# Attention 0 of a two-layer adaLN transformer: splits moved to GpSimd, a token-major output projection, and layer norm at the end of a step

## What is computed

```
mod = silu(c) @ wmod          # sa, ca, ga, ... one vector of 128 per batch
ga  = sign(ga) * max(|ga|, 0.25)
h = layernorm(x) * (1 + ca) + sa
q = h @ Wq + bq;  latent = h @ Wl + bl;  k = latent @ Wk + bk;  v = latent @ Wv + bv
attn = softmax(q k^T / sqrt(8))          # per batch, per head, 256 x 256
x = x + ga * ((attn v) @ Wo + bo)        # ga: one factor per batch and channel
```

## Time and profile before

| what | us |
|---|---|
| median of 3 runs (lowest to highest) | 968.87 (964.47 to 969.23) |
| the profiled execution, its own time | 966.18 |
| its span, from first to last instruction | 964.1 |
| preparation, until the first layer norm of attention 0 | about 21 |
| attention 0 | 21 to 343.4 |
| the three stages behind it | 343.4 to 964.1 |

### The profile page before, as it was taken

One profiled execution on the slowest core, in us unless ns is written; L12 is line 12 of the kernel. 1 busy time (PEld: TensorE's weight loads), 2 busy tenths in 40 slices (PEclk: granted clock), 3 DMA queues, 4 the chain that ended last, 5 costly groups with the idle time before them and its releaser, 6 DMA issues. The chain is left out here.

```text
span 964.1 us, 18573 instructions
## 1 busy us (share of the span) xinstructions
PE 784.2 (81%) x6147; PEld 579.6 (60%) x6160; DVE 655.9 (68%) x1698; ACT 604.1 (63%) x1371; POOL 272.2 (28%) x360
## 2 busy tenths in 40 slices
PE   3458888888688855899999964799998948999997
PEld 3213444443343335899989963678787835777775
DVE  3156777777478365777777635799999765665664
ACT  0216777777477744788888852577787835555553
POOL 3442242423120001000000004334454322555554
PEclk9999999999799975999999995899999967999999
DMA  4354435336842000000000000000000000000000
GB/s 128 41 59 51 52 47 54 45 54 86 179 51 32 3 0 1 1 2 1 2 1 1 1 2 0 1 2 1 2 2 1 2 1 1 12 11 12 23 12 22
DMA packets 42592, 24.13 MB, mean 25 GB/s; under 512 B 6169, under 2 KB 40577, under 8 KB 42497
## 3 DMA queue, kind: packets, MB, share of 16 engines
q1 hardware_dynamic: 42496, 22.92, 15.6%
HBM read 7.84 MB, written 2.10 MB: 10 GB/s over the span
## 5 line engine op out<-in xcount | busy, mean ns | idle before, releaser
L559 DVE TENSOR_REDUCE att_negmax<-att_p_max 128x2 f32<-128x512 f32 x256 | 164.6, 685 | 83.8 <-PE att_p_max L439 82.8
L643 ACT ACTIVATE att_probs<-att_p_sT 128x1024 f32<-128x1024 f32 x128 | 129.3, 1021 | 55.0 <-PE att_p_sT L445 54.1
L439 PE MATMUL att_p_max<-att0p_QK 48*128 48x256 bf16 x512 | 91.5, 289 | 36.1 <-DVE att_negmax L559 11.8
L2046 POOL TENSOR_TENSOR moe_z_lo<-moe_z,moe_z_hi 128x512 fp32r<-128x512 f32 x64 | 82.5, 1289 | 82.4 <-ACT moe_z_hi L2000 82.4
L445 PE MATMUL att_p_sT<-att0p_QK 51*128 51x256 bf16 x512 | 85.4, 278 | 1.3 <-DMA att0p_QK<-att_maxT 1.3
L439 PEld LDWEIGHTS att_p_max<-att0p_QK 48*128 48x128 bf16 x512 | 33.4, 96 | 86.1 <-DVE att_negmax L559 46.9
L2033 DVE TENSOR_TENSOR moe_act_u<-moe_act_g,moe_p_u 128x512 f32<-128x512 f32 x64 | 44.0, 687 | 59.5 <-PE moe_p_u L928 59.5
L2017 ACT ACTIVATE moe_act_g<-moe_p_g 128x512 f32<-128x512 f32 x64 | 38.3, 598 | 70.3 <-PE moe_p_g L928 69.7
L924 PE MATMUL ffn0s_p_h<-ffn0s_u_hi,ffn_h_hi 128*128 128x256 f32 x256 | 69.5, 307 | 13.5 <-DVE ffn0s_u_lo L1189 13.0
L468 PE MATMUL att_p_o<-att_probs,att0p_V 128*32 128x256 f32 x1024 | 70.2, 393 | 9.5 <-ACT att_probs L643 8.4
L1189 DVE TENSOR_TENSOR ffn0s_g_lo<-ffn0s_g,ffn0s_g_hi 128x512 fp32r<-128x512 f32 x64 | 43.2, 691 | 38.7 <-ACT ffn0s_g_hi L1134 37.5
(11 more groups left out here) (296 smaller groups left out, 2337.1 us busy)
## 6 DMA issues: line engine op xcount, KB each, us to landing
att0p_QK<-att_parts SPq DMA_DIRECT2D x192, 64.0 KB
top_X<-in_L_attn_x SPq DMA_DIRECT2D x4, 512.0 KB, 6.9
top_raw_ffn<-in_L_ffn_h_w SPq DMA_DIRECT2D x2, 1024.0 KB
out_x<-top_X SPq DMA_DIRECT2D x8, 256.0 KB, 2.3
prep_wmod<-in_L_wmod SPq DMA_DIRECT2D x2, 384.0 KB, 3.7
top_raw_ffn<-in_L_ffn_w_w SPq DMA_DIRECT2D x3, 256.0 KB
att0p_QK<-att_maxT SPq DMA_DIRECT2D x32, 12.0 KB
top_raw_moe<-in_L_ffn_w SPq DMA_DIRECT2D x1, 512.0 KB
```

The source lines that it names most:

```text
L439: mm = pe.matmul(p_max[u % 2][:, i, :], QK[r][rows, g, 0, i * P:(i + 1) * P], QK[r][rows, g, 1, :], start=True, stop=True)
L559: dve.tensor_reduce(negmax[:, :, w, g], p_max[u % 2][:], AX.X, ALU.max, negate=True).then_inc(maxed, 1)
L643: act.activation(probs[g % 2][:, t % 2], p_sT[t % 2][:], ACT.Exp).then_inc(exped, 1)
L2046: pool.tensor_tensor(z_lo[e % RING][:], z[e % RING][:], z_hi[e % RING][:].bitcast(F32), ALU.subtract).then_inc(z_lo_ready, 1)
```

## The change

- The slots move: `qk` to slot 0 on PE, `ln` to slot 15 and for the next batch (f+1), on ACT `qk` to slot 1 and `maxT` to slot 3, and `hT` of the next batch behind all slots of a step. On DVE `stats` goes to slot 0 and `add` to slot 14. `max_turn` now waits for q and k of batch f (`qk_ready`) where it waited for `hT_ready`.
- The first of the three parts of q and k goes from ACT (L625) to POOL, and so do the four instructions on the maxima (L565 to L571), with `negmax` doubled. POOL's list in a step is now: maxima, parts, normalise, weights.
- The output projection is token-major: `OTn` is the stationary operand and `Wo` of the batch the moving one, with its columns already multiplied by the gates, and a matmul of a row of ones with the gated bias row adds the bias. `yT`, its instruction on ACT and the last transpose go away.
- The gates reach that layout through a DRAM tensor: at the start of attention 0 SP stores 128 x 16 values of 4 bytes, waits for them, and loads them back to all 128 partitions (1 MB). POOL multiplies `Wo` and the bias row of one batch per step.

```diff
+PES = {"qk": 0, "max_turn": 2, "O0": 5, "v": 8, "O1": 9, "back": 11, "out": 12, "ln": 15,
        "pv_s": (11, 15), "pv_t": (3, 7)}
-DVE = {"negmax": 0, "stats": 2, "O0": 6, "O1": 10, "add": 15}
-ACTS = {"hT": 0, "maxT": 1, "qk": 3, "v": 7, "OTn": 11, "y": 12, "OT_s": (11, 15), "OT_t": (3, 6)}
+DVE = {"stats": 0, "O0": 6, "O1": 10, "add": 14}
+ACTS = {"qk": 1, "maxT": 3, "v": 7, "OTn": 11, "OT_s": (11, 15), "OT_t": (4, 6)}
...
-            pe.matmul(p_c[:, 0:1], k.wo0[:], bv_col[:], start=True, stop=True).then_inc(bo_made, 1)
+            pe.matmul(p_c[0:1, 0:D], bv_col[:], k.wo0[:], start=True, stop=True).then_inc(bo_made, 1)
...
         def pe_qk(pe, b):
             pe.wait_ge(hT_ready, b + 1)
-            at_least(pe, maxT_ready, b - 2)
...
         def pe_max_turn(pe, b):
             pe.wait_ge(neg_ready, b + 1)
-            if not isinstance(b, int) or b + 3 < B:
-                wait_apart(pe, k, hT_ready, b + 4)
+            if b + 3 < B:
+                pe.wait_ge(qk_ready, b + 4)
...
         def pe_out(pe, b):
             pe.wait_ge(OTn_ready, b + 1)
-            pe.matmul(p_m[:, 0:S], k.wo0[:], OTn[:], start=True, stop=True).then_inc(y_made, 1)
-
-        def pe_turn_y(pe, b):
-            pe.wait_ge(yT_ready, b + 1)
+            pe.wait_ge(wo_ready, b + 1)
             for i in range(NT):
-                mm = pe.transpose(p_m[:, i * P:(i + 1) * P], yT[:, i * P:(i + 1) * P], k.ident[:])
-            mm.then_inc(y_turned, 1)
+                out = p_m[:, i * D:(i + 1) * D]
+                pe.matmul(out, OTn[:, i * P:(i + 1) * P], k.wo0_all[:, b, :], start=True, stop=False)
+                mm = pe.matmul(out, k.ones_row[0:1, :], k.gbo0_row[0:1, b, :], start=False, stop=True)
+            mm.then_inc(y_made, 1)
...
-                if slot == PES["ln"] and batch_valid(f):
-                    pe_ln(pe, f)
+                if slot == PES["ln"] and batch_valid(f + 1):
+                    pe_ln(pe, f + 1)
...
-                        elif batch_valid(s):
+                        if batch_valid(s):
                             pe.wait_ge(maxT_ready, s + 1)
...
         def dve_max_tile(dve, b, u):
             g, w = u // 2, u % 2
             if u == 0:
-                at_least(dve, neg_step, 3 * (b - 1) + 2)
+                at_least(dve, neg_step, 3 * (b - 2) + 2)
...
         def dve_add(dve, b):
-            dve.wait_ge(y_turned, b + 1)
+            dve.wait_ge(y_made, b + 1)
...
             act.activation(qk[:, 1, :], p_m[:, S:2 * S], ACT.Identity, bias=k.bk0[:, 0:1]).then_inc(qk_ready, 1)
-            act.wait_ge(qk_ready, b + 1)
-            at_least(act, stacked, 16 * STACK_DMAS * (b - 1))
-            act.activation(parts[r % 2][:, :, 0], qk[:], ACT.Copy).then_inc(part0_ready, 1)
...
-                if slot == ACTS["hT"] and batch_valid(f):
-                    act_hT(act, f)
...
                 if slot in ACTS["OT_t"] and batch_valid(t):
                     act_OT(act, t, 2 + ACTS["OT_t"].index(slot))
+            if batch_valid(f + 1):
+                act_hT(act, f + 1)
...
         def pool_parts(pool, b, r):
 
+            pool.wait_ge(qk_ready, b + 1)
+            at_least(pool, stacked, 16 * STACK_DMAS * (b - 1))
+            pool.tensor_copy(parts[r % 2][:, :, 0], qk[:]).then_inc(part0_ready, 1)
...
+        def pool_wo(pool, b):
+            if b == 0:
+                pool.wait_ge(k.ga0_loaded, 16)
+            pool.tensor_tensor(k.gbo0_row[:, b, :], k.wo0_all[0:1, b, :], k.bo0_row[:], ALU.mult).then_inc(gbo_ready, 1)
+            pool.wait_ge(gbo_ready, b + 1)
+            pool.tensor_tensor(k.wo0_all[:, b, :], k.wo0_all[:, b, :], k.wo0[:], ALU.mult).then_inc(wo_ready, 1)
+
         def pool_step(pool, n, r):
+            if batch_valid(n - 3):
+                pool_negmax(pool, n - 3)
+            if batch_valid(n):
+                pool_parts(pool, n, r)
             if batch_valid(n + 1):
                 pool_normalise(pool, n + 1)
-            pool_parts(pool, n, r)
+            if batch_valid(n - 2):
+                pool_wo(pool, n - 2)
...
         @block.sync
         def _(sp):
+            sp.dma_start(k.ga0_dram.rearrange("b d -> d b"), k.mod[:, 0, GA, :], allow_slow_non_contiguous=True
+                         ).then_inc(k.ga0_stored, 16)
+            sp.wait_ge(k.ga0_stored, 16)
+            sp.dma_start(k.wo0_all[:], k.ga0_dram.rearrange("(o b) d -> o b d", o=1).to_broadcast([P, B, D])
+                         ).then_inc(k.ga0_loaded, 16)
             for n in range(WHOLE.start):
                 sp_step(sp, n, n % NB)
```

More of the change, by code:

```diff
@@ L42 @@
 SROWS = MAXROW + 3
-PES = {"ln": 0, "max_turn": 2, "qk": 3, "O0": 5, "v": 8, "O1": 9, "back": 11, "out": 12, "turn_y": 14,
+PES = {"qk": 0, "max_turn": 2, "O0": 5, "v": 8, "O1": 9, "back": 11, "out": 12, "ln": 15,
        "pv_s": (11, 15), "pv_t": (3, 7)}
-DVE = {"negmax": 0, "stats": 2, "O0": 6, "O1": 10, "add": 15}
-ACTS = {"hT": 0, "maxT": 1, "qk": 3, "v": 7, "OTn": 11, "y": 12, "OT_s": (11, 15), "OT_t": (3, 6)}
+DVE = {"stats": 0, "O0": 6, "O1": 10, "add": 14}
+ACTS = {"qk": 1, "maxT": 3, "v": 7, "OTn": 11, "OT_s": (11, 15), "OT_t": (4, 6)}
 F = 512
@@ L183, in _ @@
                                  allow_slow_non_contiguous=True).then_inc(small_loaded, 16)
-            for n, name in ((2, "L0_attn_bv"), (3, "L0_attn_bo")):
-                sp.dma_start(cols[:, n:n + 1], a[name].rearrange("(d o) -> d o", o=1)).then_inc(small_loaded, 16)
+            sp.dma_start(cols[:, 2:3], a["L0_attn_bv"].rearrange("(d o) -> d o", o=1)).then_inc(small_loaded, 16)
+            sp.dma_start(bo_row[:], a["L0_attn_bo"].rearrange("(o d) -> o d", o=1)).then_inc(small_loaded, 16)
             for n, name in enumerate(("L0_wmod", "L1_wmod")):
@@ L341, in attention0 @@
         parts = [sb(f"parts{n}", [P, 2, 3, S], BF16) for n in range(2)]
-        negmax = sb("negmax", [P, NT, 2, PAIRS])
+        negmax = [sb(f"negmax{n}", [P, NT, 2, PAIRS]) for n in range(2)]
         negrest = sb("negrest", [P, NT, 2, PAIRS])
@@ L536, in pe_step @@
                     pe_out(pe, t)
-                if slot == PES["turn_y"] and batch_valid(t):
-                    pe_turn_y(pe, t)
         def dve_stats(dve, b):
@@ L597, in dve_step @@
             for slot in range(TILES):
-                if slot == DVE["negmax"] and batch_valid(s):
-                    dve_negmax(dve, s)
                 if slot == DVE["O0"] and batch_valid(t):
@@ L653, in act_OTn @@
             act.activation(OTn[:], p_m[:, 0:S], ACT.Copy).then_inc(OTn_ready, 1)
-        def act_y(act, b):
-            act.wait_ge(y_made, b + 1)
-            at_least(act, y_turned, b)
-            act.activation(yT[:], p_m[:, 0:S], ACT.Identity, bias=k.gbo0[:, bass.ds(b, 1)],
-                           scale=k.mod[:, 0, GA, bass.ds(b, 1)]).then_inc(yT_ready, 1)
         def act_step(act, n, r):
@@ L674, in act_step @@
                     act_OTn(act, t)
-                if slot == ACTS["y"] and batch_valid(t):
-                    act_y(act, t)
                 if slot >= 6 and slot % 2 == 0 and batch_valid(s):
@@ L777, in _ @@
                     pool_step(pool, turn * NB + (WHOLE.start + r), r)
-            for n in range(WHOLE.stop, B):
+            for n in range(WHOLE.stop, B + 3):
                 pool_step(pool, n, n % NB)
@@ L782, in _ @@
         def _(pe):
+            pe_ln(pe, 0)
             for n in range(WHOLE.start):
@@ L792, in _ @@
         def _(act):
+            act_hT(act, 0)
             for n in range(WHOLE.start):
@@ L2101, in build @@
         k.wq0, k.wk0, k.wv0, k.wo0 = (sb(f"w{x}0", [P, D]) for x in "qkvo")
-        k.bq0, k.bk0, k.bo0 = (sb(f"b{x}0", [P, 1]) for x in "qko")
-        k.gbo0 = sb("gbo0", [P, B])
+        k.bq0, k.bk0 = (sb(f"b{x}0", [P, 1]) for x in "qk")
+        k.bo0_row = sb("bo0_row", [1, D])
+        k.ones_row = sb("ones_row", [1, P])
         k.ffn_scales = sb("ffn_scales", [P, 4, FB])
@@ L2119, in build @@
         k.late_loaded = sem("late_loaded")
+        k.ga0_dram = nc.dram_tensor("gates0", (B, D), F32, kind="Internal").ap()
+        k.ga0_stored = sem("ga0_stored")
+        k.ga0_loaded = sem("ga0_loaded")
         k.waits_passed = sem("waits_passed")
@@ L2124, in build @@
             k.V = [wsb(f"V{n}", [P, NT, H0, 32]) for n in range(NB)]
+            k.wo0_all = wsb("wo0_all", [P, B, D])
+            k.gbo0_row = wsb("gbo0_row", [1, B, D])
             prepare(nc, k, a)
```

36 lines of the change are left out of this document (18 added, 18 removed).

## The result

The changed kernel took **1070.1 us** (median of 4 runs, 1068.12 to 1072.84) against 967.0 for the kernel before (median of 4 runs beside it). The ratio is 1.1063, with a 95% interval of 1.1034 to 1.1092: slower by 103 us, where I forecast 1018, so 51. The direction and the waits were as forecast. The size was double.

A forecast was written before the change was run, and what follows sets the result against it. PE's in-order list, about 14.4 us of work plus waits, was taken to set each step; +4.3 in 11 steps plus smaller terms gave +50.7 on 966.18, 1016.9, forecast as 1018 us, range 1001 to 1036.

The forecast's parts named there:

- the walk: One full step of attention 0 in the new order: 16.67 to 20.95 us, +4.3, with 6.6 of new PE waits.
- POOL's split: Four instructions on the maxima on POOL: 1.2 us, bounds 0.8 and 2.4, hidden in the wait before the turn.
- rival A: In attention 0's steps waits drop TensorE's clock: about 2 us more per step, 12 steps, 1042 us; chance 0.10.
- step 13: Attention 0's step with late weight loads: 2.5 us of the 9 us stall stays, so −6.5, bounds 0 and −9.
- the projection's length: Attention 0's output projection as eight matmuls: 1.14 us, bounds 1.0 and 1.42, where two took 0.70.
- Start: Gates' store and load ahead of the first sp_stack: +3 us, and 0.4 for ln of batch 4; bounds 0 and 12.
- Rival D: The gates' store and load at the start cost the upper bound, 12 us: 1027 us; chance 0.12.
- Tail: Attention 0's steps 16 to 18, without q and k: +1.4 us each, +4.2; last step −0.7.
- Rivals B: Faster: waits of max_turn and tile 6 cost nothing, about 1 us goes in each of 12 steps, 954; chance 0.06.
- C: No change: only waits at a step's start and before layer norm remain, +0.4 in each of 12 steps, 967; chance 0.04.
- E: POOL's split does not hide, only if it takes over 4 us; inside the forecast's range, no separate chance given.
- worth nothing: In attention 0's steps, what is taken off DVE and ACT lay beside PE's work and gains nothing.

The follow-up runs named there:

- Runs 5: Changed kernel with ACT making q and k, maxT and hT earlier and DVE adding to x at slot 12: 1009.8 us.
- run 9: Changed kernel with q and k put back behind the turn of the maxima, maxT at ACT slot 1: 1007.0 us.
- run 12: Changed kernel with q and k back behind the maxima's turn, hT and the addition earlier, and the gated bias as bf16 rows: 961.5 us, ratio 0.9936.
- run 1: Changed kernel with filler matmuls, read by nothing, that PE runs in its four waits: 1040.7 us.
- run 6: Kernel before with the token-major projection, less its two 1-row matmuls for the gated bias (output lacks that bias): 969.4 us.
- run 3: Kernel before with only the token-major projection, its weights' products and the gates' transfers: 1002.5 us.
- run 7: Kernel before with only the gates' store and load at the start and one POOL wait for the load: 969.9 us, ratio 1.0016.
- run 4: Kernel before with only the first split of q and k and the four instructions on the maxima on POOL: 964.8 us, ratio 0.9965.
- run 8: Kernel before with the token-major projection and the splits on POOL, without the new order of the step: 988.0 us.
- runs 2: Changed kernel with ACT copying q and k ahead of the exponential of slot 0: 1070.5 us.

## Why the prediction was wrong in size

**Right: the walk.** The waits came where it put them, with the releasers it named: 0.95 forecast and 0.96 measured before q and k, 1.85 and 1.93 to 1.97 before the turn, 2.35 and 2.34 before tile 6 in a warm step, 1.45 and 1.58 before layer norm. At full clock the step is 21.7, against 20.95. POOL's split hid entirely (its four instructions take 1.13 with gaps; I had taken 1.2). Runs 5, 9 and 12 show that the waits are the cause by taking them away.

**Wrong: the clock, put at nothing in the sum.** This is the step that failed: the sum priced every step at full clock, and left the low one to rival A, at a chance of 0.10. I argued from the earlier trace rows that PE kept its clock through a stretch with little work, and compared only the longest single wait (2.35) with the 7.85 of step 13. The trace of the changed kernel has half of a step at 0.50. Run 1 measures it at 29 us at least, since the clock still fell a little there; by steps it is 3.2 each (24.9 against 21.7), where A had 2. The earlier trace rows were the wrong rows: they cover one short stretch with no wait over 0.74, and say nothing of waits of up to 2.3 that come back in each of twelve steps. The Trainium skill (TensorE: Matmul & The Clock Gate, "Why this matters for your kernels") warns of idle gaps that halve the clock. The trace agrees that idle gaps bring it down, since filling them brought it back (run 1), but it does not take one long gap, as that advice reads: the longest here is 2.34. I had added that the rival would hold only if the waits ran together; the waits here stay apart, by up to 8.5 us of work (224.49 to 232.96), and the clock falls all the same.

**Wrong: the projection's length.** I took 1.14, with bounds of 1.0 and 1.42; it is 1.73. My upper bound was twice the 0.71 of two matmuls of 128 rows in a row, and my figure lay below it, as if a row of one cost less. In the alternation each kind costs 0.42, and the two ones-rows add 1.02 between them (run 6). That is 0.59 in each step, 8 us in 14 steps in the forecast's terms. Its real price was higher: alone on the kernel before it took 35 us (run 3), all but 2 of it gone without the rows (run 6), since it also lets the clock fall in steps that had just kept it.

**Nothing lost, nothing gained: step 13.** I kept 2.5 of the 9 of stall and credited 6.5. The stall went entirely (25.97, like its neighbours), so my bound of −9 was the better number; its gain is in the table only as the smaller growth of that step.

**Start.** I had +3 for the transfers, within 0 to 12, up to tile 6 of step 3; it came 2.0 later. The store took 10.6 rather than some 7, but SP had room for most of it. Rival D wasn't it: run 7 puts the transfers at 2 us of the total, not told from none. The advice against a strided last dimension (the Trainium skill, DMA: Bandwidth & Descriptors, "Rules for kernel authors") fits the transfer, with 10.0 to 11.5 us for 8 KB, though no run stores the same bytes in a row; the kernel's time hardly shows it. The first addition came 2.7 later than forecast, though tile 6 of step 3 came 1.4 earlier than forecast; the difference lies in step 4, where tiles still take 0.37 at 99 us (in the kernel before the last such one is at 81).

**Tail.** I had +1.4 each for steps 16 to 18; they took +4.9, +4.0 and +2.3, at granted clocks like 0.88 in step 18. In the last step the gain of 0.7 became a loss of 1.3.

**The sum, repaired.** Of the 52 us missed: some 35 for the clock in eleven full steps (3.2 each), 8 for the projection. The table's other differences, in the tail above all, make up the rest; how much of those is clock I didn't separate. Rivals B, C and E did not occur. What leaves DVE and ACT I had as "worth nothing" but for pv3's wait of 0.62, and in a step of the kernel before that wait is all that went (0.4 to 0.65, run 4); on top of the projection it was worth 14 us (run 8), since there it also kept the clock up.

**What stays open.** No run tells what about the waits makes the clock fall, their sum or their spacing. Nor did I find why the same step in run 9 takes 17.94, 19.07 and 21.02 in turn. The statistics at slot 0 on DVE, which tile 3 waits for in runs 2 and 5, were not moved back in any run with q and k ahead of the turn. How much of run 12's gain is the splits', the cheaper list or the earlier layer norm was not tried apart.
